# Attention heads of eight rows each: two heads on the two partition halves, six of nine product terms, all heads gathered at once

## The reference, cut to what matters

```
scores = q @ k.T / sqrt(8)          # q, k: 2048 x 8
weights = softmax(scores)           # causal mask in one of the four
out = weights @ v
```

## Time and profile before

| | us |
|---|---|
| median of 3 runs (lowest, highest) | 4514.57 (4512.73, 4515.37) |
| the profiled execution | 4526.3 |
| its span | 4524.5 |
| busy: TensorE, VectorE, ScalarE, GpSimd | 3962.3, 3194.4, 2199.4, 97.5 |

### The profile page before, as it was taken

How to read it: one execution, slowest core, us unless ns; L and a number is a source line. 1 busy time by engine, 2 the same in 40 slices (tenths; PEclk the granted TensorE clock), 3 DMA queues, 4 the chain that set the end, 5 groups by cost and what they waited for, 6 DMA issues and landing times.

```text
span 4524.5 us, 59451 instructions
## 1 busy us (share of the span) xinstructions
PE 3962.3 (88%) x22108; PEld 1619.8 (36%) x22108; DVE 3194.4 (71%) x6776; ACT 2199.4 (49%) x2694; POOL 97.5 (2%) x59
## 2 busy tenths in 40 slices
PE   5989797599999984999999986399894899999986
PEld 3756655122222232222222363133232232222253
DVE  5256255688888835888888548486774888888546
ACT  2222321166666651466666721156473266666721
POOL 0000000200000001000000001100001000000000
PEclk8889898599999995799999988599897699999988
DMA  0011500100000002000000000100001000000000
GB/s 23 4 43 25 116 1 6 70 1 22 2 22 2 2 6 77 12 2 22 22 2 1 20 1 0 70 2 23 22 2 47 24 2 22 11 13 2 1 19 10
DMA packets 37282, 87.42 MB, mean 19 GB/s; under 512 B 7080, under 2 KB 31432, under 8 KB 32200
## 3 DMA queue, kind: packets, MB, share of 16 engines
q1 hardware_dynamic: 36856, 82.09, 5.7%
q10 hardware_dynamic: 144, 1.53, 0.1%
HBM read 68.91 MB, written 14.70 MB: 18 GB/s over the span
## 4 chain that ended last, share of the span: by engine, by line
PE 75%; DVE 16%; DMA 3%; ACT 2%; SPq 2%; issue 2%; POOL 0%; ACTq 0%; DVEq 0%
PE ps L1767 18%; PE ps L1752 18%; PE ps L1732 15%; DVE pm L1817 8%; PE ps L945 3%; PE ps L948 3%; PE ps L2058 3%; PE ps L1024 3%; PE ps L2034 3%; SPq L1308 2%; DMA m_dram<-mt 1%; PE ps L1458 1%; DVE XN L289 1%; PE ps L1208 1%; PE ps L744 1%
## 5 line engine op out<-in xcount | busy, mean ns | idle before, releaser
L1817 DVE TENSOR_REDUCE pm<-ps 128x1 f32<-128x512 f32 (+2 forms) x3712 | 2258.9, 669 | 453.6 <-PE ps L1732 413.8
L1793 ACT ACTIVATE arena<-ps 128x1024 f32<-128x1024 f32 x1728 | 1684.8, 1022 | 791.5 <-PE ps L1752 788.1
L1732 PE MATMUL ps<-arena 72*128 72x512 bf16 (+2 forms) x3712 | 1453.5, 398 | 154.3 <-DMA arena<-parts_dram 127.6
L1752 PE MATMUL ps<-arena 75*128 75x512 bf16 (+1 forms) x3712 | 1385.7, 382 | 57.1 <-DMA arena<-m_dram 52.1
L1767 PE MATMUL ps<-arena,VA 128*16 128x512 f32 (+2 forms) x7424 | 965.7, 592 | 0.0
L1752 PEld LDWEIGHTS ps<-arena 75*128 75x128 bf16 x3712 | 357.1, 98 | 1098.6 <-issue 771.5
L1732 PEld LDWEIGHTS ps<-arena 72*128 72x128 bf16 x3712 | 368.6, 100 | 672.9 <-DVE pm L1817 338.0
L1767 PEld LDWEIGHTS ps<-arena,VA 128*16 128x16 f32 x7424 | 122.9, 94 | 310.8 <-issue 299.8
L976 DVE TENSOR_TENSOR arena<-EV,ps 128x512 f32<-128x512 f32 x128 | 87.8, 686 | 125.4 <-PE ps L948 120.8
L964 ACT ACTIVATE EV<-ps 128x512 f32<-128x512 f32 x128 | 76.2, 597 | 203.5 <-PE ps L945 203.5
L945 PE MATMUL ps<-XNT,arena 128*128 128x512 f32 x304 | 160.9, 612 | 2.3 <-DVE arena L1251 1.5
(11 more groups left out here) (263 smaller groups left out, 2795.6 us busy)
## 6 DMA issues: line engine op xcount, KB each, us to landing
arena<-parts_dram SPq DMA_DIRECT2D x72, 384.0 KB
parts_dram<-parts SPq DMA_DIRECT2D x32, 384.0 KB, 3.4
arena<-k_dram SPq DMA_DIRECT2D x20, 528.0 KB, 11.2
arena<-parts_dram SPq DMA_DIRECT2D x96, 96.0 KB
parts<-k_dram SPq DMA_DIRECT2D x8, 528.0 KB, 6.4
arena<-in_w SPq DMA_DIRECT2D x4, 1024.0 KB, 6.2
VA<-k_dram SPq DMA_DIRECT2D x4, 528.0 KB, 7.4
arena<-in_w12T SPq DMA_DIRECT2D x1, 2048.0 KB, 13.2
```

What stands on the lines that cost most here:

```text
L1732: ins = e.matmul(bank[:, 0:w], QP[0:KR, g % 2, hh, i * P:(i + 1) * P], KP[0:KR, g % 2, hh, kc * CH:kc * CH + w], start=True, stop=not diag)
L1752: ins = e.matmul(bank[:, off:CH], KP[0:KM, g % 2, hh, j * P:(j + 1) * P], QP[0:KM, g % 2, hh, q * CH + off:(q + 1) * CH], start=True, stop ...
L1793: e.activation(self.PB[:, pb, :, :], c.bank(2 * k, 2).rearrange("p (a t) -> p a t", a=2), ACT.Exp, scale=self.scale).then_inc(self.exped.s ...
L1817: e.tensor_reduce(c.pm[:, u % 2, hh * TPC + qt, kc:kc + 1], self.slot_bank(slot)[:, 0:w], AX, ALU.max).then_inc(self.emptied.sem, 1)
```

## The change

- Of the nine pairs of parts six are left, (0,0), (0,1), (0,2), (1,0), (1,1), (2,0) as (part of q, part of k): 48 rows instead of 72, 51 with the rows of maxima. Even heads use partitions 0 to 50 and odd heads 64 to 114, so that a pair of heads' matmuls use the upper and the lower half of the array's rows.
- All 16 heads' rows fit in SBUF now (`packed`: 8 pairs x 2048 tokens x q and k). `gather_rows` gathers a chunk of all heads with 12 DMAs (q or k, half, and three, two or one terms); the gathers in `Heads` are gone, and `Heads` waits for the last one at its start. The channels' order in the weights (`by_parity`), the buffers of `Prepare` (two chunks in turn instead of all tokens), the rotary tables (twice as wide) and `Temper` (five steps instead of seven) follow.
- A tick is one key tile of a pair of heads. Scores: two matmuls, one for each half, then the exponential of both. Maxima: even and odd head in turn, each still in one single bank with one reduction. Values follow after each key tile. `LEAD` is 9, the turning of maxima and outputs comes four ticks after their request instead of three.
- GpSimd splits the maxima; ScalarE copies the turned rows out; the DMA back is two, one for each half.

```diff
-TERMS = SPLIT * SPLIT
+Q_PARTS = (0, 0, 0, 1, 1, 2)
+K_PARTS = (0, 1, 2, 0, 1, 0)
+TERMS = len(Q_PARTS)
...
-def gather_rows(e, c, g, t0, n, marks):
-    QP, KP = packed(c)
-    slot = g % 2
-    for a in range(SPLIT):
-        rows = slice(SPLIT * HD * a, SPLIT * HD * (a + 1))
-        for dst, which, first, step in ((QP, 0, a, 0), (KP, 1, 0, P * T)):
-            src = bass.AP(tensor=c.parts_dram.tensor,
-                          offset=(which * SPLIT + first) * P * T + g * HD * GH * T + t0,
-                          ap=[[step, SPLIT], [GH * T, HD], [T, GH], [1, n]])
-            e.dma_start(dst[rows, slot, :, t0:t0 + n], src).then_inc(marks.sem, 16)
+def gather_rows(e, c, t0, n, marks):
+    for w, rows in enumerate(packed(c)):
+        for par in range(2):
+            for term, part, step in ((0, 0, w), (3, 1 - w, w), (5, 2 * (1 - w), 0)):
+                n_terms = {0: 3, 3: 2, 5: 1}[term]
+                src = bass.AP(tensor=c.parts_dram.tensor,
+                              offset=(w * SPLIT + part) * P * T + par * (P // 2) * T + t0,
+                              ap=[[step * P * T, n_terms], [PAIRS * T, HD], [T, PAIRS], [1, n]])
+                first = par * (P // 2) + term * HD
+                e.dma_start(rows[first:first + n_terms * HD, :, t0:t0 + n], src).then_inc(marks.sem, 16)
...
     def maxima(self, u):
-        steps = [(u, hh, qt, kc) for hh in range(GH) for qt in range(TPC)
-                 for kc in range(k + 1 if self.causal else NC)]
+        steps = [(u, pp, qt, kc, par) for pp in range(2) for qt in range(TPC)
+                 for kc in range(k + 1 if self.causal else NC) for par in range(2)]
...
-                    for jj in range(2):
-                        self.steps.append(("scores", u, hh, pair[jj], jj, self.exps))
-                        for _ in range((n + 1) // 2 if jj == 0 else n // 2):
-                            self.run(pending.pop(0))
-                    self.steps.append(("exp", u, hh, pair, self.exps))
+                    self.score_pair(u, j, pp)
+                    for _ in range(n):
+                        self.run(pending.pop(0))
                     self.tick()
+                waiting.append((u, j, first, j == n_keys - 1))
+                if len(waiting) > 1:
+                    self.values(*waiting.pop(0))
...
     def tensor(self, e):
+        e.wait_ge(*self.gathered)
...
-                ins = e.matmul(bank[:, 0:w], QP[0:KR, g % 2, hh, i * P:(i + 1) * P],
-                               KP[0:KR, g % 2, hh, kc * CH:kc * CH + w], start=True, stop=not diag)
+                rows = slice(64 * par, 64 * par + KR)
+                ins = e.matmul(bank[:, 0:w], QR[rows, 2 * g + pp, i * P:(i + 1) * P],
+                               KT[rows, 2 * g + pp, kc * CH:kc * CH + w], start=True, stop=not diag)
                 if diag:
                     ins = e.matmul(bank[:, w - P:w], c.IDB[:, :], c.MQB[:, :], start=False, stop=True)
...
+                for par in range(2):
+                    rows = slice(64 * par, 64 * par + KM)
+                    ins = e.matmul(c.bank((t + par) % 4)[:, off:CH], KT[rows, 2 * g + pp, j * P:(j + 1) * P],
+                                   QR[rows, 2 * g + pp, q * CH + off:(q + 1) * CH], start=True, stop=not diag)
                 if diag:
-                    ins = e.matmul(bank[:, off:off + P], c.IDB[:, :], c.MKB[:, :], start=False, stop=True)
+                    for par in range(2):
+                        ins = e.matmul(c.bank((t + par) % 4)[:, off:off + P], c.IDB[:, :], c.MKB[:, :], start=False,
+                                       stop=True)
```

More of the change, by code:

```diff
@@ L1579, in run @@
                 self.steps.append(("finish", u))
-                self.later.append([3, ("rows", u)])
+                self.later.append([4, ("rows", u)])
         else:
@@ L1591, in tick, with keys, score_pair, values @@
                 self.run(item[1])
-    def batches(self, k):
-        n = TPC * (k + 1) if self.causal else NT
-        return [(j, j + 1) for j in range(0, n, 2)]
-    def offsets(self, k, pair):
-        return [max(0, (j - TPC * k) * P) if self.causal else 0 for j in pair]
-    def values(self, items, u, last):
-        for jj in range(2):
-            self.steps.append(("values", u, jj, items, last))
-            yield
+    def keys(self, k):
+        return TPC * (k + 1) if self.causal else NT
+    def score_pair(self, u, j, pp):
+        q = self.units[u][1]
+        off = max(0, (j - TPC * q) * P) if self.causal else 0
+        first = self.tiles
+        self.tiles += 2
+        self.tile_off += [off, off]
+        self.steps.append(("scores", u, j, pp, first))
+        while len(self.exp_of) < self.tiles:
+            t = len(self.exp_of)
+            n = 2
+            self.exp_of += [self.exps] * n
+            self.steps.append(("exp", t, n, self.exps))
+            self.exps += 1
+    def values(self, u, j, first, last):
+        self.steps.append(("values", u, j, first, last))
         if last:
+            self.last_tile[u] = first + 3
             self.steps.append(("empty", u))
-            self.later.append([3, ("out", u)])
+            self.later.append([4, ("out", u)])
     def lay_out(self):
         units = self.units
-        self.steps.append(("gather", 1))
         for step in self.maxima(0):
@@ L1615, in lay_out @@
         for _, k in units:
-            starts.append(starts[-1] + len(self.batches(k)) * GH)
-        pending, reached, queued, total, clock, waiting = [], 0, [], 0, 0, None
+            starts.append(starts[-1] + 2 * self.keys(k))
+        pending, reached, queued, total, clock = [], 0, [], 0, 0
+        waiting = []
         for u, (g, k) in enumerate(units):
-            if u % NC == 0 and 1 <= g < NG - 1:
-                self.steps.append(("gather", g + 1))
-            todo = self.batches(k)
-            for b, pair in enumerate(todo):
-                items = []
-                for hh in range(GH):
+            n_keys = self.keys(k)
+            for j in range(n_keys):
+                first = self.tiles
+                for pp in range(2):
                     while reached < min(u + 2, len(units) - 1):
@@ L1767, in tensor @@
+                for hh in range(GH):
                     ins = e.matmul(c.bank(4)[32 * hh:32 * hh + VW, off:CH], c.VA[:, j, GH * g + hh, :],
-                                   self.PB[:, n % self.PBS, jj, off:CH], start=j == 0, stop=last and jj == 1,
+                                   self.PB[:, (first + hh) % self.PBS, off:CH], start=j == 0, stop=last,
                                    tile_position=(0, 32 * hh))
-                    if jj == 1:
-                        ins.then_inc(self.valued.sem, 1)
+                ins.then_inc(self.valued.sem, 1)
@@ L2403, in layout @@
     return {
+        "ones": np.full((1, PAIRS * T // 2), ONE_PAIR, np.float32),
         "x": i["L0_attn_input_data"].reshape(T, P),
```

340 lines of the change are left out of this document (170 added, 170 removed).

## The result

| | before | after |
|---|---|---|
| median, us (4 runs each, one chip) | 4514.97 | 4714.65 |
| lowest, highest | 4512.73, 4523.97 | 4710.74, 4725.9 |
| span of the profiled execution | 4524.5 | 4708.9 |

The ratio is 1.0442, 95% interval 1.0419 to 1.0466: 200 us slower. The forecast was 4592 us, 78 slower: the direction is right, the size is wrong by 122 us. The time lies in the wide range (4430 to 4745) and outside the one given to the forecast itself (4535 to 4650). From profile to profile the span grew by 184.4 us. The four stretches between stages of heads grew by 73.0, 71.2, 69.9 and 69.8, together 284; the three stages without a mask lost 31.1, 31.7 and 35.1, together 98; the masked stage lost 0.8 and all the rest 0.9. 284 - 98 - 1.7 = 184.3.

A forecast was written before the change was run, and what follows sets the result against it. TensorE was taken to bound the body before, a three-bank loop after; -87 (units) - 13 (ends) - 54 (masked stage) + 224 (gathers) + 6 + 2 = +78 us, so 4592 us; own range 4535 to 4650, wide range 4430 to 4745.

The forecast's parts named there:

- Steady units: Body of unmasked stages: a loop through three banks sets 2.69 us a key tile, 44.4 a unit; -87 us.
- (b): Body of unmasked stages: the loop doesn't close, VectorE runs back to back; -289 instead of -87, 4390 us; chance 0.07.
- (c): Paired heads' matmuls on row halves don't overlap; +60 instead of -87, 4755 us; chance 0.10.
- Ends of these stages: First and last key tiles of the three unmasked stages: small gains, ScalarE bounding the last ones; -13 us.
- the starts: Start of each stage: the return copy, now two, is exposed only there; +1.5 us each, +6 in all.
- Gathers: Before each stage's heads: TensorE waits 97 us for copies queued on few engines; +56 a stage, +224 us.
- rival (a): Gathers don't bound, copies run side by side on other engines; +7 a stage instead of +56, 4396 us; chance 0.12.
- eight engines, 0.35 us: Gathers: a one-term copy spreads its eight rows over eight engines and takes 0.35 us, against 2.7 on one.
- Masked stage: The stage with masks: waits for rows of maxima go (-36), some 8 us less half clock, -10 rest; -54 us.
- I take -10 for the rest: Masked stage: overlap gains against full-height masks' tiling changes; -10 us, between -50 (all hidden) and +50 (all paid).
- GpSimd: Splitting of maxima moved from VectorE: five steps at 0.4 us each, covered by four ticks; at 1.15 us each, +60.
- rival (e): Less busy TensorE loses full clock: past 5500 us if it stays at half, partly 100 to 300 us; chance 0.05.

The follow-up runs named there:

- e1: Changed kernel with only a key tile's order changed: two maxima, both score pairs, two maxima, values; 4535.91 us, unit period 41.06 us.
- e9: Changed kernel with the six gather copies of the second row half issued from ScalarE's queue instead of SyncE's; 4705.13 us.
- e2: Changed kernel with a chunk's twelve gather copies made into 24 copies of one term, 8 rows, 64 KB each; 4559.89 us.
- h1: Changed kernel with the masked stage's mask matmuls replaced by 64-row ones adding zeros, so diagonal tiles stay unmasked; 4663.67 us, masked stage 480.5 us.
- j1: Changed kernel with diagonal masks computed in full on each head's own 64-row half, triangle stationary, unit matrix moving; 4662.09 us, masked stage 484.3 us.
- e5: Changed kernel with all mask matmuls of the masked stage left out, so diagonal tiles stay unmasked; 4662.41 us, masked stage 476.9 us.

## Why the prediction was wrong in size

- **Steady units: right.** 44.4 forecast, 44.37 measured, key tile 2.69 as summed from the links of the earlier trace rows. Rivals (b) and (c) are out: VectorE waits 0.20 us in a key tile, and two heads' scores take one slot (2201.79 to 2202.02). e1 shows the loop by changing it.
- **Ends of these stages: right.** -87 and -13 less 4.5 for the starts were forecast, -98 measured; the last key tiles have ScalarE busy 32.75 of 35 us, as said.
- **Gathers: the mechanism held, the term was mis-sized.** The copies queue on few engines (rival (a) is out by the DMA share of 0.19, and by e9), and the pace of three and of two engines is in the windows. The step that failed is the 5.75 us of a set of three kinds, "eight engines, 0.35 us" for its one-term copy with it: a set takes 6.62 us, 0.87 more, and sixteen sets make 14 of the 16 us between the 97 forecast and the 113.2 measured. The first engine's 136 KB at the 24 GB/s of the long stretches account for 5.9 of the 6.62 us; the rest goes where the pace drops, most plainly to 38 GB/s for 0.8 us behind the one-term copy's burst. The prediction had taken the engines' rate as constant. Why it drops stays open; e2 shows that copies of this size among their like take 0.70 us or less, and the trace doesn't name the engines. The stretches between stages grew by 284 instead of 226 (with the tables' 2): 58 us of the miss.
- **Masked stage: the step "I take -10 for the rest" failed.** The waits went (all left are 5.2 us), as said. But 256 diagonal maxima and 128 diagonal score pairs now have masks on all 128 rows among matmuls on 64, and that cost 53 us of the stage, measured by h1, which only halves the masks' height. The rest should have carried +43 and not -10, 52 us of the miss. The price itself was read rightly: 0.09 forecast, 0.09 to 0.10 at each change of the maxima. A pair of diagonal maxima with its masks took 2 x (0.22 + 0.06) = 0.56 us before and takes 0.95 now; 128 such pairs would be 50 us, an estimate from these rows. What failed is the cover that -10 took for granted: in this stage TensorE is busy 501 of 533 us. And the sum had no term for the slots that the masks keep a pair's maxima from sharing (0.28 us in j1). The rule of "TensorEngine Tiling (Array Packing)", Key Properties, in the Trainium skill, that a change of tiling mode drains TensorE, was the better guide, and by it the forecast would have been 4648. That h1's stage is 53.4 us shorter than that of the kernel before, just the forecast's -54, is in part luck: 8 of the 54 were to come from less half clock, and the granted clock fell instead.
- **GpSimd: right.** Its five steps take 0.20 to 0.25 us each (0.4 taken); the units' period shows that none of them is waited for in the body.
- **The reference point.** Of the rest 15 us are the reference point: the profiled execution of before was 12 us above its median, that of after 4 below.
- **Clock (rival (e)): not in the body**, 1.00 there with TensorE busy 260 of 300 us. In the masked stage it fell from 0.90 to 0.84; what that costs stays open, beyond that h1 and j1 win 53 and 49 us of the stage at 0.85.

## What to carry to other kernels

Where an engine is nearly always busy, a small price at each of hundreds of instructions isn't hidden: here 56 of the 108 us that e5's expectation counted for the masks showed in the stage. Look for it before the long waits, and for another form of the operation that doesn't pay it (here stationary and moving operands exchanged). Copies don't spread over idle DMA engines by themselves: look at the outermost loop first (three, two and one terms kept the DMA share at 0.19, 48 rows brought it to 1.12, and that paid although the data are stored twice). In a loop through few buffers, count the longest stretch in which none of them is filled, and break it up by reordering before adding buffers.

## What was not expected of the hardware

- 64-row matmuls, back to back for 117 of 120 us, left the granted clock at 0.50 (1.2 GHz); with full-height ones it was 0.75 over the first 40 us.
- Taking 512 masks out of the kernel before gained nothing clear of noise (-3 us): its masked stage's granted clock fell from 0.90 to 0.83.
- Half of the copies on a second queue: with ScalarE's the wait is 110 to 112 us, with GpSimd's 78 to 87.
- Changing between 64 and 128 rows cost TensorE 0.1 us each way, more than the 0.06 us of the 128-column mask itself.
- Behind each one-term copy of a mixed set the few engines at work dropped to 38 GB/s for 0.8 us, some 14 GB/s for each busy one where they have 22 to 24 otherwise.
